# A broadcast row written to memory from SBUF columns instead of by transpose and copy

## The reference

```python
h = jnp.maximum(_layernorm(x, axis=-1), 0.0)
x = x + _L0_gnn_ref(h, adj, L0_gnn_W, L0_gnn_a)     # ends in an ELU
h = jnp.maximum(_layernorm(x, axis=-1), 0.0)
x = x + _L1_gnn_ref(h, adj, L1_gnn_W, L1_gnn_a)     # no ELU

# a layer, for each graph:
Wh = h @ W
e1 = Wh @ a1;  e2 = Wh @ a2
e = e1[:, :, None] + e2[:, None, :]
e = jnp.where(e > 0, e, 0.2 * e)                    # leaky ReLU
attention = softmax(jnp.where(adj > 0, e, neg), axis=2)
out = attention @ Wh
```

## Time and profile before

| | us |
|---|---|
| median of 3 timed runs | 313.43 (313.27 to 316.34) |
| profiled execution, its own time | 314.74 |
| its span, first to last instruction | 312.9 |

### The profile page before, as it was taken

How to read it: one execution, slowest core, us unless ns; L and a number is a source line. 1 busy time by engine, 2 the same in 40 slices (tenths; PEclk the granted TensorE clock), 3 DMA queues, 4 the chain that set the end, 5 groups by cost and what they waited for, 6 DMA issues and landing times.

```text
span 312.9 us, 6581 instructions
## 1 busy us (share of the span) xinstructions
PE 293.6 (94%) x2560; PEld 288.6 (92%) x2560; DVE 267.3 (85%) x610; ACT 164.5 (53%) x485; POOL 47.6 (15%) x53
## 2 busy tenths in 40 slices
PE   7999779799899999999999999999999999789695
PEld 7899679799899999999999999999999999788595
DVE  4596389949999989999899989999899959919785
ACT  3284480784493747483583648382674654353200
POOL 2612001220303030303003030303002000400000
PEclk9999999999999999999999999999999999999999
DMA  7997495102574334904574345713491302001211
GB/s 248 410 405 317 154 389 197 67 2 68 190 244 175 138 134 151 384 7 142 195 310 162 138 135 189 284 68 115 161 356 47 138 0 70 0 0 40 96 69 67
DMA packets 15247, 50.56 MB, mean 162 GB/s; under 512 B 2040, under 2 KB 3056, under 8 KB 15216
## 3 DMA queue, kind: packets, MB, share of 16 engines
q1 hardware_dynamic: 14640, 49.75, 43.0%
q10 hardware_dynamic: 576, 0.39, 0.4%
HBM read 45.88 MB, written 4.26 MB: 160 GB/s over the span
## 4 chain that ended last, share of the span: by engine, by line
PE 74%; DVE 10%; DMA 4%; ACT 4%; issue 4%; POOL 2%; POOLq 0%; DVEq 0%; ACTq 0%
PE acc L790 55%; PE prj L750 7%; PE tp L693 4%; DVE pbuf L564 4%; DMA row_r<-r_rows 3%; PE acc L806 2%; PE acc L690 2%; ACT xn L349 2%; POOL rstd L254 2%; DMA r_rows<-rT 1%; DVE stats L476 1%; DVE x_sb L594 1%; DVE ex L588 1%; PE prj L753 1%; DVE accs L573 1%
## 5 line engine op out<-in xcount | busy, mean ns | idle before, releaser
L790 PE MATMUL acc<-wh,pbuf 128*128 128x129 f32 x1984 | 232.9, 276 | 10.1 <-DVE accs L573 8.1
L790 PEld LDWEIGHTS acc<-wh,pbuf 128*128 128x128 f32 x1984 | 227.0, 192 | 13.3 <-issue 9.9
L564 DVE SCALAR_TENSOR_TENSOR pbuf<-row_r,sqr,adj_sb 128x1024 f32<-128x1024 f32 x127 | 157.8, 1278 | 8.8 <-DMA row_r<-r_rows 8.8
L254 POOL TENSOR_TENSOR rstd<-vareps,neg_half 128x8 f32<-128x8 f32 x15 | 37.5, 2503 | 213.9 <-DVE vareps L494 213.8
L379 ACT ACTIVATE accs<-accs,rec 128x128 f32<-128x128 f32 x120 | 36.7, 390 | 59.3 <-DVE rec L583 59.3
L349 ACT ACTIVATE xn<-x_sb,shift,rstd 128x128 f32<-128x128 f32 x120 | 47.6, 480 | 0.0
L368 ACT ACTIVATE wh<-prj,wh 128x128 f32<-128x128 f32 x120 | 31.6, 350 | 0.0
L750 PE MATMUL prj<-w_ext,hT 128*128 128x130 f32 x240 | 29.4, 275 | 0.1
L750 PEld LDWEIGHTS prj<-w_ext,hT 128*128 128x128 f32 x240 | 28.0, 191 | 0.2 <-ACT hT L355 0.2
L573 DVE TENSOR_TENSOR accs<-acc,uniform 128x387 f32<-128x387 f32 (+1 forms) x48 | 22.0, 508 | 4.2 <-PE acc L790 2.0
L476 DVE BATCH_NORM_STATS2 stats<-x_sb 128x6 f32<-128x128 f32 x120 | 24.6, 279 | 0.0
(11 more groups left out here) (81 smaller groups left out, 146.1 us busy)
## 6 DMA issues: line engine op xcount, KB each, us to landing
adj_sb<-in_adj SPq DMA_DIRECT2D x64, 512.0 KB, 6.5
row_r<-r_rows SPq DMA_DIRECT2D x15, 512.0 KB, 3.9
x_sb<-in_x SPq DMA_DIRECT2D x7, 512.0 KB, 7.1
out_x<-x_sb SPq DMA_DIRECT2D x7, 512.0 KB, 3.0
out_x<-x_sb SPq DMA_DIRECT2D x2, 192.0 KB, 1.9
x_sb<-in_x ACTq DMA_DIRECT2D x1, 256.0 KB, 3.6
x_sb<-in_x SPq DMA_DIRECT2D x1, 256.0 KB, 3.4
r_rows<-rT SPq DMA_DIRECT2D x15, 4.0 KB
```

The source lines that it names most:

```text
L254: nc.gpsimd.tensor_tensor(rstd[:, :], vareps[:, :], neg_half[:, :], ALU.pow).then_inc(rstd_ready, 1)
L564: nc.vector.scalar_tensor_tensor(pbuf[:, t, :], row_r[:, n % 2, :], sqr[:, n % 2, 0, t:t + 1], adj_at(b, t), ALU.max, ALU.min).then_inc(p_ ...
L790: mm = nc.tensor.matmul(acc[:, k, s * C:(s + 1) * C], pbuf[:, t, i * P:(i + 1) * P], wh[:, n % 2, t, :], start=(t == 0 and s == 0), stop=( ...
```

## The change

The row's write no longer goes through PE and ACT. SP writes r as it lies in `sqr`: 128 partitions with 8 numbers (32 bytes) each, one behind the other in memory, so the row that comes back is in order of the nodes (p * 8 + t) instead of tile by tile. The masks then read it with a step of 8 words, as 8 runs of 128, so that `pbuf` keeps its order; the other two operands are written as 8 runs of 128 too, with a step of one word. Stage 0's row, made on the chip, stays tile by tile. `turn_r`, `copy_r`, the tile `rT` and their two semaphores are gone; `transposes` waits for `cmax_ready` instead of `rT_ready`.

```diff
             def load_row(m):
-                sp.wait_ge(rT_ready, m)
-                sp.dma_start(r_rows, rT[:, :]).then_inc(r_written, 16)
+
+                sp.wait_ge(sqr_ready, m + 1)
+                sp.dma_start(r_rows.rearrange("t p -> (t p)").rearrange("(p t) -> p t", t=T),
+                             sqr[:, m % 2, 2, :]).then_inc(r_written, 16)
                 sp.wait_ge(r_written, 16 * m)
...
-            def copy_r(m):
-                act.wait_ge(r_turned, m)
-                nc.scalar.activation(rT[:, :], tp[0:T, 0:P], ACT.Copy).then_inc(rT_ready, 1)
...
                     exps(n + 1)
-                    copy_r(n + 1)
...
+            def row_at(n):
+
+                row = row_r[:, n % 2, :]
+                return (row.rearrange("q (t p) -> q t p", t=T) if n == 0
+                        else row.rearrange("q (p t) -> q t p", t=T))
+
+            def by_tile(columns):
+                return columns.rearrange("q (t p) -> q t p", t=T)
+
...
-                    nc.vector.scalar_tensor_tensor(pbuf[:, t, :], row_r[:, n % 2, :],
-                                                   sqr[:, n % 2, 0, t:t + 1], adj_at(b, t),
+                    nc.vector.scalar_tensor_tensor(by_tile(pbuf[:, t, :]), row_at(n),
+                                                   sqr[:, n % 2, 0, t:t + 1],
+                                                   by_tile(adj_at(b, t)),
                                                    ALU.max, ALU.min).then_inc(p_ready, 1)
...
-                    pe.wait_ge(rT_ready, m - 1)
+                    pe.wait_ge(cmax_ready, m)
...
-            def turn_r(m):
-                pe.wait_ge(sqr_ready, m + 1)
-                nc.tensor.transpose(tp[0:T, 0:P], sqr[:, m % 2, 2, :],
-                                    ident[:, :]).then_inc(r_turned, 1)
...
                     spread_emax(n + 1)
-                    attend(n, (4,))
-                    turn_r(n + 1)
-                    attend(n, (5,))
+                    attend(n, (4, 5))
                 else:
                     project(n + 1)
                     attend(n, (0,))
                     spread_emax(n + 1)
-                    attend(n, (1,))
-                    turn_r(n + 1)
-                    attend(n, (2, 3, 4, 5))
+                    attend(n, (1, 2, 3, 4, 5))
```

More of the change, by code:

```diff
@@ L60, in gat_two_layers @@
         gate = sb("gate", [P, 1])
-        rT = sb("rT", [T, P])
         act_gate = sb("act_gate", [P, 1])
@@ L146, in gat_two_layers @@
         q_ready = sem("q_ready")
-        r_turned = sem("r_turned")
-        rT_ready = sem("rT_ready")
         r_written = sem("r_written")
@@ L835, in _ @@
             spread_emax(1)
-            attend(0, (4,))
-            turn_r(1)
-            attend(0, (5, 6))
+            attend(0, (4, 5, 6))
             transposes(2)
```

## The result

The changed kernel takes 394.35 us (median; 392.06 to 396.82) against 313.84 us for the kernel before (313.27 to 316.34) in the runs compared with it. The ratio is 1.255 [1.248, 1.261]: 80.5 us slower. The forecast was 311.3 us and the range ended at 360 us, so the time lies outside of the range, on the side of the first rival.

What follows compares the result with a forecast made beforehand. PE was taken to bound the middle, with DVE close behind, and the row's load stages 1 and 15. Ten transposes 1.1 + stage 15 1.0 + stage 1 0 = 2.1 us, so 313.4 - 2.1 = 311.3 us; range 309.8 to 360 us.

Steps and rivals of the forecast that it cites:

- the first rival: All 120 masks of line 564: the stride slows them; about 359 us (chance 0.18 up to there) or 420 us (0.16).
- the price of the stride: Masks of stages 1 to 15 reading the row at 32-byte steps: 0 to 1.05 us more per mask, taken as 0.
- p = 0.5 us: p is the stride's price per mask; at 0.5 us, from `mdiff`, 48 us more, so about 359 us.
- the formula: A pair of stages grows by 16p - 0.94 us, five pairs in the middle; the ends add 30 masks' price less 2 us.
- "DVE's only idle time": In a pair of middle stages, DVE idles only while waiting for a projection: 1.16 us in 34.80 us.
- The rule of lines of 16 bytes: Masks' SBUF reads: full speed needs two hits per 16-byte line; a 32-byte step takes a new line every time; no price given.
- The ten transposes: PE between 81 and 255 us: ten `turn_r` transposes of 0.11 us leave the chain, 1.1 us gained.
- The write at stage 15: Last row's write: starts 1.3 us sooner, takes 1.5 us, 0.3 us more than before; 1.0 us gained.
- Stage 1: Its row's write is issued 1.0 us sooner but sits behind adjacency loads; gain between 0 and 1.0 us, taken as 0.

Runs made afterwards that it cites:

- The probes: The kernel before, with single instructions of various lengths, steps, operands and engines placed behind its last result; 335.73 us including them.
- the run of steps: The kernel before, but in stages 1 to 15 the mask of tile t reads the row with a step of 2^t words; 366.59 us in one run.

## Why the prediction was wrong

**The step that failed is the price of the stride**, "I take 0: `q_rstd` is nearest". It measures 0.80 us per mask. The bounds, 0 to 1.05 us, hold it; the choice between the ends was made by the row whose step was most like the change's, although its length, 8 elements, was least like it. The probes show what that hid: the first eight elements or so are free. The prediction called the basis thin, "eight elements in an instruction of 160 ns", and still gave it 0.66 of the chance. `mdiff`, whose 4 ns over 8 elements spoke the other way, wasn't the evidence it looked like: in the probe 8 elements cost nothing more, so those 4 ns are not shown to be the stride's.

**The range** ended at p = 0.5 us, which left p up to 1.05 us outside with a chance of 0.16. With two ends and no row of a long strided read in between, nothing in the trace said that 0.5 was more likely than 0.8.

**The rival's mechanism was right.** DVE became the bound of every stage. With p = 0.80 us the formula gives 5 x (16 x 0.80 - 0.94) = 59.3 us for the middle and 30 x 0.80 - 2 = 22 us for the ends, 81.3 us on top of the 311.3 of the forecast, so 392.6 us; 394.35 were measured. For the middle the runs bear it out: per stage it gives 8 x 0.80 - 0.47 = 5.9 us, and the windows 23.2 - 17.29 = 5.9 against the stage without the stride. The 22 us of the ends were an estimate that no run divides, and 2.6 us of clock in them (last section) are not in the formula; that the whole comes out so near is in part luck. "DVE's only idle time", 1.16 us, was a misreading of the earlier trace rows, which have 1.72 us in a pair; it matters for two strided masks, not for 16. The rule of lines of 16 bytes, which the prediction put beside this rival, is borne out (the run of steps).

**The ten transposes** were right: stages of 17.29 us without the stride, 0.11 less than before.

**The write at stage 15** was mis-sized. It starts where the step said, 0.02 us behind the exponentials. But the write took 2.14 us (without the stride) and 2.51 us (with it), not 1.5, so from the end of the exponentials to the load's issue the time fell from 285.86 + 1.21 - 284.53 = 2.54 us to 288.45 - 286.27 = 2.18 without the stride: 0.4 us gained, not 1.0. In quiet middle stages it takes 1.40 us, close to the forecast; why it takes longer in stage 15, where in the changed kernel the DMA share is 0.00 in the microsecond before and 0.06 during the write, stays open.

**Stage 1**, taken as 0, scattered around it. From the end of the exponentials to the load's issue it took 32.20 - 27.74 = 4.46 us before, 31.26 - 27.55 = 3.71 us in the changed kernel and 33.04 - 28.28 = 4.76 us without the stride. So for the change without its stride the terms are 1.1 + 0.4 - 0.3 = 1.2 us; measured were 0.0046 x 315.09 = 1.4 us, with an interval of 0.1 to 2.8.

## What to carry to other kernels

Price a change of access pattern from an instruction of the same length, and where there is only a short one, take the bound from the other end as just as likely: eight elements can be free where 1024 cost 0.8 us. A layout that has to be mended should be mended once, by an engine with time to spare, and not in each of its readers; and before anything is put on the engine next to the bound, what it can use of its idle time is the budget, here 1.3 us for 16 masks. Work taken from the bound (here ten transposes of 0.11 us) is small change beside that.

## What the runs showed of the hardware

- VectorE, float32, two inputs: a step of 2 words is free. At 128 elements a step of 3 words costs 33 ns and steps of 4 to 8 words 85 to 92 ns; at 1024 elements steps of 4 to 128 words cost 686 to 814 ns, 0.67 to 0.79 ns per element, without growth in the step. It doesn't matter whether one input, both, or the output has the step. From PSUM there was no price.
- The reads of SBUF that were tried on other engines pay too. 1024 elements in order and by step 8: VectorE with one input 682 and 1075 ns, ScalarE 1056 and 2031, GpSimd 2783 and 3754; a TensorE weight load 192 and 336.
- The write in pieces of 32 bytes alternates in the middle of the changed kernel between 1.40 us and 2.1 to 3.8 us, stage by stage: the longer ones come behind three adjacency loads in the queue, at a DMA share of 0.41 to 0.59 during the write against 0.05 to 0.06.
- TensorE's clock fell where TensorE had to wait. The changed kernel's PE row behind one such wait, and the windows beside it:

```profile
139.05 3.26 PE L787 MATMUL acc<-wh,pbuf 128*128 128x129 f32 x16 [2.89 <-DVE accs L575]
...
139.00:141.00 2.00, 1.95 (x11) 1.98 (x12) 1.93 (x8) 1.03 (x4) 0.00 (x0) 0.65 0.79 254
141.00:143.00 2.00, 2.00 (x12) 2.00 (x11) 1.86 (x3) 1.42 (x5) 0.00 (x0) 0.50 0.12 47
```

After 2.89 us without work the granted clock is 0.65 and then 0.50, the lower of its two levels (1.2 GHz). In that stage it comes with the loss and doesn't make it: DVE is busy for 22.23 of 22.54 us. At the end it costs time, because PE's last matmuls are on the chain. The last 46 in the changed kernel with their window, and the same 46 in the run with one strided mask, at full clock:

```profile
383.36 8.01 PE acc L803 x46
...
384.00:388.00 4.00, 4.00 (x20) 4.00 (x20) 1.61 (x5) 0.00 (x0) 0.00 (x0) 0.50 0.07 28
...
306.50 5.42 PE acc L803 x46
```

PE had waited for masks three times before them and worked for 4.18 of the 8 us from 376 to 384. The difference is 2.6 us.
- GpSimd's `rstd` took 3101 ns in the mean in the changed kernel against 2503 before, with no change in its code. Its single instructions show why: 1.64 us where DVE started no mask just before it (at 63.13 us in the kernel before), 2.6 us behind a mask of 1.28 us, 3.3 to 3.4 us behind a strided one. A longer mask on DVE makes it longer by about as much. In the changed kernel it wasn't on the path.
